# Preparation of an attention and expert kernel on one Trainium2 core: semaphores per transfer, other staging buffers, another order

## What is computed

```python
x = x + tanh(g_xattn) * xattn(layernorm(x), ctx, ctx, Wq, bq, Wk, bk, Wv, bv, Wo, bo)
# xattn: q = xn @ Wq + bq ; k = ctx @ Wk + bk ; v = ctx @ Wv + bv ; 16 heads of 32
#        softmax(q k^T / sqrt(32)) v, joined, @ Wo + bo          (ctx: 2 x 128 x 256)
x = x + tanh(g_ffn) * moe(layernorm(x))
# moe: LayerNorm with gamma, beta; logits = xn @ router_w.T; top 2 of 8 experts;
#      each expert takes up to 1280 rows: h = silu(g) * u, y = h @ w3.T, weighted and added
```

## Time and profile before

| | before |
|---|---|
| median of 3 runs | 2720.58 us (2719.67 to 2720.80) |
| the profiled execution's own time | 2716.51 us |
| its span in the trace | 2714.10 us |
| TensorE matmul busy | 2608.7 us (96%) |
| VectorE busy | 1392.1 us (51%) |
| ScalarE busy | 944.7 us (35%) |
| GpSimd busy | 410.9 us (15%) |

### The profile page before, as it was taken

The page is one execution under the profiler, slowest core; times in us unless marked ns, Lnnn a source line. Parts: engine busy times, 40 slices in busy tenths (PEclk is TensorE's granted clock), DMA queues, the critical chain, the costliest instruction groups (busy, mean ns, idle before and its releaser), DMA issues.

```text
span 2714.1 us, 40566 instructions
## 1 busy us (share of the span) xinstructions
PE 2608.7 (96%) x14166; PEld 2313.9 (85%) x14167; DVE 1392.1 (51%) x2647; ACT 944.7 (35%) x2479; POOL 410.9 (15%) x391
## 2 busy tenths in 40 slices
PE   5999999589999999999999999999999999999988
PEld 4877777489998888888988888888889999989987
DVE  4788888544444444444444444444444444445555
ACT  4766666222224222242222322232222322233343
POOL 2455555400002000020000300010000100030030
PEclk8999999799999999999999999999999999999999
DMA  7523222321103201132011321141011311033142
GB/s 266 213 78 102 94 78 97 122 111 47 46 27 77 86 24 46 47 62 86 23 46 46 63 109 46 47 113 40 30 46 39 107 47 46 33 85 118 70 126 81
DMA packets 60034, 208.38 MB, mean 77 GB/s; under 512 B 9564, under 2 KB 9836, under 8 KB 51602
## 3 DMA queue, kind: packets, MB, share of 16 engines
q1 hardware_dynamic: 43282, 175.30, 18.0%
q0 software_dynamic: 16640, 31.69, 6.1%
HBM read 145.60 MB, written 67.70 MB: 79 GB/s over the span
## 4 chain that ended last, share of the span: by engine, by line
PE 76%; issue 2%; DVE 1%; ACT 1%; DVEq 0%; DMA 0%; ACTq 0%; POOL 0%; POOLq 0%
PE bank L1540 75%; PE bank L1546 1%; DVE yacc L1480 1%; DVE slotsT_lo L1449 0%; ACT slotsT_hi L1372 0%; DVE h L1500 0%; DMA xrow<-expert_rows 0%; ACT later_hi L1368 0%; ACT yout L1396 0%; ACT h_hi L1410 0%; POOL out_dram L1354 0%; DVE w_lo L1443 0%; DVEq L1252 0%; ACT silu L1404 0%; DVEq L1479 0%
## 5 line engine op out<-in xcount | busy, mean ns | idle before, releaser
L1500 DVE TENSOR_TENSOR h<-silu,bank 128x384 f32<-128x384 f32 (+2 forms) x320 | 183.8, 574 | 826.3 <-PE bank L1540 816.8
L1540 PE MATMUL bank<-slotsT_hi,early_hi 128*128 128x384 f32 (+2 forms) x1280 | 444.6, 347 | 14.4 <-issue 12.3
L1540 PE MATMUL bank<-slotsT_hi,w_hi 128*128 128x384 f32 (+2 forms) x1280 | 442.5, 346 | 5.3 <-DVE w_lo L1443 5.3
L1540 PE MATMUL bank<-slotsT_lo,early_hi 128*128 128x384 f32 (+2 forms) x1280 | 442.5, 346 | 0.4 <-issue 0.4
L1540 PE MATMUL bank<-slotsT_lo,w_hi 128*128 128x384 f32 (+2 forms) x1280 | 442.2, 345 | 0.0
L1540 PE MATMUL bank<-slotsT_hi,early_lo 128*128 128x384 f32 (+2 forms) x1280 | 441.8, 345 | 0.0
L1540 PE MATMUL bank<-slotsT_hi,w_lo 128*128 128x384 f32 (+2 forms) x1280 | 441.1, 345 | 0.0
L1410 ACT CAST h_hi<-h 128x384 fp32r<-128x384 f32 (+2 forms) x320 | 169.2, 529 | 745.9 <-DVE h L1500 743.0
L1404 ACT ACTIVATE silu<-bank 128x384 f32<-128x384 f32 (+2 forms) x320 | 162.0, 506 | 728.8 <-PE bank L1540 728.3
L1480 DVE TENSOR_TENSOR yacc<-bank,yacc 128x512 f32<-128x512 f32 x464 | 316.6, 688 | 169.0 <-PE bank L1540 169.0
L1540 PE MATMUL bank<-later_hi,h_hi 128*128 128x512 f32 x1008 | 399.8, 397 | 0.3 <-DVE yacc L1480 0.3
(11 more groups left out here) (195 smaller groups left out, 3533.3 us busy)
## 6 DMA issues: line engine op xcount, KB each, us to landing
staged<-in_moe_w_dram SPq DMA_DIRECT2D x33, 1536.0 KB
raw<-in_moe_w_dram SPq DMA_DIRECT2D x32, 1536.0 KB, 6.4
xrow<-expert_rows SPq DMA_DIRECT2D x42, 520.0 KB, 9.0
expert_rows<-zeros SPq DMA_DIRECT2D x40, 520.0 KB, 7.5
xin<-in_x_dram SPq DMA_DIRECT2D x17, 512.0 KB, 3.7
xres<-in_x_dram SPq DMA_DIRECT2D x15, 512.0 KB, 3.7
out_dram<-xres SPq DMA_DIRECT2D x15, 512.0 KB
staged<-in_L_xattn_Wq_dram SPq DMA_DIRECT2D x1, 1024.0 KB, 10.7
```

The source lines that it names most:

```text
L1500: nc.vector.tensor_tensor(h32[q % 2][:, 0:W], silu[q % 2][:, 0:W], UB[q % 2][:, 0:W], ALU.mult)\
L1540: last = nc.tensor.matmul(out_ap, st, mv, start=(at == 0), stop=(at == n - 1))
```

## The change

Each transfer, or small group, gets its own semaphore. x of block 0 is issued first, then context, router weights and biases, `Wk`, `Wq`, `Wo`, `Wv`, `bv`, the gates. The biases are loaded as four rows of 128 into the residual's buffer and turned by PE. Raw `Wk`, `Wv` and `Wo` lie in `pT`, `Wq` alone in `probs`. `Wq` is rounded and split in four pieces. x is turned ahead of the keys; only batch 0's keys are made before the first queries, batch 1's behind them. The values are made inside block 0, batch 1's keys are split by POOL in block 0, and `Wo`'s subtraction moves to a later place in block 0.

```diff
-                    for dst, src in kv_parts:
-                        sp.dma_start(dst, src, allow_slow_non_contiguous=True).then_inc(kv_loaded, 16)
                     load_xin(0)
+                    for dst, src in ((row[:, :, 0:DI], ctx_img.rearrange("b s d -> s b d")),
...
+                                     (bias_rows[0:KD, 0, 0:P], bk.rearrange("(m p) -> m p", p=P)),
+                                     (bias_rows[0:KD, 1, 0:P], bq.rearrange("(m p) -> m p", p=P))):
+                        sp.dma_start(dst, src).then_inc(ctx_loaded, 16)
+                    sp.dma_start(wk_raw, wide(Wk)).then_inc(wk_loaded, 16)
                     sp.dma_start(wq_raw, wide(Wq)).then_inc(wq_loaded, 16)
-                    load_xres(0)
+                    sp.dma_start(wo_raw, wide(Wo)).then_inc(wo_loaded, 16)
+                    sp.dma_start(wv_raw, wide(Wv)).then_inc(wv_loaded, 16)
+                    sp.dma_start(bv_row[:, :], bv.rearrange("(a n) -> a n", a=1)).then_inc(wv_loaded, 16)
+                    for i, g in enumerate((g_xattn, g_ffn)):
+                        sp.dma_start(gates[:, i:i + 1], g.partition_broadcast(P), allow_slow_non_contiguous=True)\
+                          .then_inc(gates_loaded, 16)
+
+                    sp.wait_ge(x_ready, 2)
+                    load_xin(1)
                     for dst, src in ((gbo_b, bo), (gamma_b, ln_gamma), (beta_b, ln_beta)):
                         sp.dma_start(dst[:, :], src.partition_broadcast(P)).then_inc(late_loaded, 16)
-                    sp.wait_ge(x_ready, 2)
-                    load_xin(1)
-                    sp.wait_ge(prep_pe, 3)
-                    sp.dma_start(wo_raw, wide(Wo)).then_inc(wo_loaded, 16)
+                    load_xres(0)
...
@@ POOL
+                    for t in (k_hi[0], k_lo[0]):
+                        last = nc.gpsimd.memset(t[:, :, :].bitcast(fp32), 0.0)
+                    last.then_inc(k0_cleared, 1)
                     rstd_x(0)
+                    for t in k_hi[1:] + k_lo[1:]:
...
+                    def later_keys():
+                        pool.wait_ge(cleared, 2)
+                        pool.wait_ge(k1_biased, KD)
+                        pool.wait_ge(pn_ready, KD - 1)
+                        for i, (rows, cols) in enumerate(diagonal):
+                            nc.gpsimd.tensor_copy(k_hi[1][rows, :, cols], keys(1, rows)).then_inc(k1_rounded, 1)
+                            pool.wait_ge(k1_rounded, i + 1)
+                            nc.gpsimd.tensor_tensor(k_lo[1][rows, :, cols], keys(1, rows),
+                                                    k_hi[1][rows, :, cols].bitcast(fp32), ALU.subtract).then_inc(k1_split, 1)
...
                         if has(n, 0):
                             norm(n, 2)
+                        if isinstance(n, int) and n == 0:
+                            later_keys()
@@ ACT
                     norm_x(0)
                     act.wait_ge(wq_loaded, 16)
-                    nc.scalar.copy(wq_hi[:, :, :], wq_raw).then_inc(prep_act, 1)
+                    for k in range(KD):
+                        nc.scalar.copy(wq_hi[:, k, :], wq_raw[:, k, :]).then_inc(wq_rounded, 1)
                     x_halves(0)
...
+                    act.wait_ge(wo_loaded, 16)
+                    nc.scalar.copy(wo_hi[:, :, :], wo_raw).then_inc(wo_rounded, 1)
+                    act.wait_ge(k0_cleared, 1)
+                    act.wait_ge(k_biased, KD)
+                    for rows, cols in diagonal:
+                        nc.scalar.copy(k_hi[0][rows, :, cols], keys(0, rows)).then_inc(k_rounded, 1)
...
                     q_halves(0, 0)
+                    act.wait_ge(k_made, 2)
+                    for m in range(KD):
+                        nc.scalar.activation(row[:, 1, m * LKV:(m + 1) * LKV], bank[5][:, m * LKV:(m + 1) * LKV],
+                                             ACT.Identity, bias=bkT[:, m:m + 1], scale=SCALE).then_inc(k1_biased, 1)
@@ DVE
+                    stats_x(0)
...
+                    for m in range(KD):
+                        nc.vector.tensor_scalar(row[:, 0, m * LKV:(m + 1) * LKV], bank[4][:, m * LKV:(m + 1) * LKV],
+                                                SCALE, bkT[:, m:m + 1], ALU.mult, ALU.add).then_inc(k_biased, 1)
...
                     q_rest(0, 0)
+                    stats_x(1)
@@ PE
                     transposes_x(0)
...
+                    keys_made(0)
+                    pe.wait_ge(wq_split, 1)
                     queries(0, 0)
+                    keys_made(1)
+                    pe.wait_ge(k0_split, 1)
...
                             queries(n, 1)
+                            if isinstance(n, int) and n == 0:
+                                values_made(0)
                             scores(n, 2, b_s)
                         if has(n, 1):
...
                             transposes_x(n + 1)
+                        if isinstance(n, int) and n == 0:
+                            values_made(1)
```

More of the change, by code:

```diff
@@ L226, in flamingo_gated_layer @@
             row_of = lambda blk: spare_row if isinstance(blk, int) and blk == LAST - 1 else row
+            keys = lambda b, rows: row[rows, b, 0:KD * LKV].rearrange("p (m t) -> p m t", m=KD)
+            diagonal = [(slice(DK * hh, DK * (hh + 1)), slice(LKV * hh, LKV * (hh + 1))) for hh in range(HG)]
             def steps(eng, step):
@@ L639, in _ @@
-                    x_rest(0)
-                    dve.wait_ge(prep_pool, 1)
-                    dve.wait_ge(prep_act, 3 + B * KD)
-                    keys = lambda b, rows: row[rows, b, 0:KD * LKV].rearrange("p (m t) -> p m t", m=KD)
-                    diagonal = [(slice(DK * hh, DK * (hh + 1)), slice(LKV * hh, LKV * (hh + 1))) for hh in range(HG)]
-                    for b in range(B):
-                        for rows, cols in diagonal:
-                            last = nc.vector.tensor_copy(k_hi[b][rows, :, cols], keys(b, rows))
@@ new lines, in _ @@
+                    nc.vector.tensor_scalar(bkT[:, :], bank[2][:, KD * E:KD * E + KD], SCALE, None, ALU.mult)
+                    nc.vector.tensor_copy(bqT[:, :], bank[2][:, KD * E + KD:KD * E + 2 * KD]).then_inc(turned_read, 1)
+                    for k in range(KD):
+                        dve.wait_ge(wq_rounded, k + 1)
+                        last = nc.vector.tensor_tensor(wq_lo[:, k, :], wq_raw[:, k, :], wq_hi[:, k, :].bitcast(fp32),
+                                                       ALU.subtract)
@@ new lines, in _ @@
+                    last.then_inc(wq_split, 1)
+                    x_rest(0)
+                    dve.wait_ge(turned_read, 1)
+                    dve.wait_ge(k_made, 1)
+                    for m in range(KD):
+                        nc.vector.tensor_scalar(row[:, 0, m * LKV:(m + 1) * LKV], bank[4][:, m * LKV:(m + 1) * LKV],
+                                                SCALE, bkT[:, m:m + 1], ALU.mult, ALU.add).then_inc(k_biased, 1)
+                    for i, (rows, cols) in enumerate(diagonal):
+                        dve.wait_ge(k_rounded, i + 1)
+                        last = nc.vector.tensor_tensor(k_lo[0][rows, :, cols], keys(0, rows),
+                                                       k_hi[0][rows, :, cols].bitcast(fp32), ALU.subtract)
@@ new lines, in _, with values @@
+                    last.then_inc(k0_split, 1)
+                    q_rest(0, 0)
+                    stats_x(1)
+                    def values():
+                        for b in range(B):
+                            dve.wait_ge(v_made, b + 1)
+                            nc.vector.tensor_copy(vals[b][:, :, :], bank[2 + b][:, :].rearrange("p (h d) -> p h d", h=H))                              .then_inc(vals_ready, 1)
+                    def late_splits():
+                        dve.wait_ge(wo_rounded, 1)
@@ L923, in _, with keys_made @@
                                                    row[0:E, a, DI + c * P:DI + (c + 1) * P], ident[0:E, 0:E])
-                    last.then_inc(prep_pe, 1)
-                    pe.wait_ge(prep_dve, 1)
+                    for i in range(2):
+                        last = nc.tensor.transpose(bank[2][:, KD * E + i * KD:KD * E + (i + 1) * KD],
+                                                   bias_rows[0:KD, i, 0:P], ident[0:KD, 0:KD])
+                    last.then_inc(turned, 1)
                     ctxT = xnT
-                    for b in range(B):
+                    def keys_made(b):
                         for m in range(KD):
```

123 lines of the change are left out of this document (52 added, 71 removed).

## The result

| | before | changed |
|---|---|---|
| median | 2720.12 us (4 runs, 2715.93 to 2720.80) | 2701.39 us (4 runs, 2698.94 to 2703.30) |
| ratio to before | | 0.9938, 95% interval 0.9927 to 0.9950 |
| the profiled execution's own time | 2716.51 us | 2701.12 us |
| its span | 2714.10 us | 2698.40 us |
| first scores, fifth scores group | 35.05, 57.19 | 20.66, 36.07 |

The medians differ by 18.7 us, where 20.0 was forecast. By the ratio the gain is 16.9 us, with an interval of 13.6 to 19.9, so the forecast lies at its upper edge. The two profiled executions differ by 15.4 (their spans by 15.7), because what follows the load of block 4's x, the same code in both, took 3.2 us longer in the second; how that stretch scatters is shown at the end of the experiments.

What follows compares the result with a forecast made beforehand. The prediction took the late start, work not yet needed and DVE's key splits to bound the head, PE's work block 0; 15.0 + 6.0 - 0.8 - 0.2 = 20.0 us less, 2720.6 to 2700.6, range 2696.5 to 2709.

Steps and rivals of the forecast that it cites:

- Bound and place: Head: late start, early work for batch 1 and values, and DVE's key splits set 35.05; 15.0 saved.
- `Wq` at 9: Head: data to the end of `Wq`, 2.3 MB at 408 GB/s, there by about 9, before ACT wants it.
- The turn of x: Head, on PE ahead of batch 0's keys: takes 1.0, to 11.1.
- Which of the two ends sets the first scores: First scores: DVE's q low part ends at 19.4, PE's batch 1 keys at 20.0, so PE's sets them.
- Block 0: First scores to fifth scores group: PE's work is the length, 16.1 for 22.1, 6.0 saved if the clock stays up.
- Rival A: Half clock stays: up to 2 in the head, some 6 in block 0; about 2707.6; chance 0.10.
- Given back: `Wo`'s low part and bias row ahead of `maxima(0, 6)` cost 0.8; POOL's delay of `norm(0, 3)` costs 0.2.
- Rival B: New late work binds: `Wo`'s subtraction and POOL's eight instructions fall together; gain 13, 2707.6; chance 0.12.
- POOL's keys: Eight key instructions ahead of `norm(0, 3)`: take 7.0, bounds 6.4 to 8.4, costing 0.2 (0 to 1.6).
- The signs: PE's first instruction near 5.5, first scores near 20, fifth group near 36, no PE idle over 1 us between.
- Rival C: Gain absorbed by slow early data or 40 zero fills ahead of the first scatter; 2715 to 2720; chance 0.04.
- D: Slower: half clock at the stage change lasts into the experts, about 2726; chance 0.02.

## Why the prediction was right

By its own steps, with what the profile of the changed kernel shows:

| step | forecast | measured |
|---|---|---|
| x landed, statistics start | 4.3 | 4.64 |
| normalisation starts | 8.5 | 8.63 |
| x turned | 10.0 to 11.1 | 10.20 to 12.17 |
| `Wq` there | 9 | 11.0 |
| queries start | 14.0 | 15.52 |
| q's low part (DVE) ready | 19.4 | 20.5 |
| batch 1's keys (PE) done | 20.0 | 20.4 |
| first scores | 20.0 (15.0 saved) | 20.66 (14.4 saved) |
| to the fifth group | 16.1 (6.0 saved) | 15.41 (6.7 saved) |
| given back | 1.0 | 2.2 at block 4's x |
| saved at block 4's x | 20.0 | 18.9 |
| medians | 20.0 | 18.7 |
| the profiled executions | 20.0 | 15.4 |

The number came out closer than its parts. Up to the fifth group an error of 0.6 and one of 0.7 cancel, and that is luck. So is part of the agreement of the median, 2701.4 for 2700.6: the profiled execution was forecast at 2696.5 and took 2701.1, since the gain was 1.1 short and the tail 3.2 longer; but the distance from it to the median, kept at 4.1, was 0.3 this time. The mechanism, what each step waits for, is what held, with the exceptions below.

- **Bound and place.** Right: one wait for all transfers held the start, and to put it back costs 10.9, or some 8 if it ended as early as in the kernel before. DVE's chain ahead of q's low part was the second bound; undoing batch 1's move costs 6.2 at the first scores and 7.9 at block 4's x. These don't add up with the others (10.9 + 7.9 + 2.8 + 1.1 = 22.7, more than 18.9), since undoing one part can also drop the clock or lengthen another wait.
- **`Wq` at 9** failed: the forecast assumed the full 408 GB/s from the start, but the queues moved 164 GB/s in 6 to 7 and 289 in 7 to 8 (the data are also 2.4 MB rather than 2.3). `Wq` was there at 11.0 and ACT waited 0.9 for it. The queries started 1.5 late. Of this, 1.0 is ACT's later start on `Wq`; the rest is DVE, which was still busy with `Wq`'s low part (from 11.68 to 14.1) when ACT had the first half of x's high part, where the forecast called that work hidden. The 0.3 by which x landed late is not in it, since ACT then waited for `Wq` all the same.
- **The turn of x** was priced at 1.0 from a row at full clock; behind PE's idle it took 1.97. It ended at 12.17, ahead of ACT's cast of x at 13.11, so this cost nothing.
- **Which of the two ends sets the first scores** came out the other way. The forecast had PE's (20.0) behind DVE's (19.4). DVE's chain was 1.1 late, with the queries, and ended last (PE waited 0.26 for it). Batch 1's keys, priced at 2.8, took 1.95 at full clock, so PE was done at 20.4 though its queries started late. The 0.66 at the first scores is what is left of the two errors.
- **Block 0** was right in kind, PE's work sets its length; 16.1 was 0.7 high, mostly because its two sets of queries took 2.88 and 2.86 and not 3.1 each. The four scores groups took 3.1 together, as forecast.
- **Rival A** (half clock) did not occur where it would have cost much: only the turn of x, the first keys and the stretch behind the wait of 2.06 were slow. Its ground, that every idle stretch before was followed by half clock, went too far: PE's 1.73 idle ahead of 43.80 in the kernel before was followed by a turn at the full rate (1.09 for eight). The undoing of batch 1's keys showed half clock once PE idles 6 us. The prediction's gain counted on PE staying busy, and it did.
- **Given back.** `Wo`'s subtraction was priced at 0.8 for pushing back `maxima(0, 6)`. The size by the next block's first scores (66.10 before, 46.13 now, so 20.0 saved where 21.1 were at the fifth group) is 1.15, but the mechanism was another one: it held POOL's work and with it `norm(0, 1)`, for which PE waited 2.06; with the subtraction moved away, the wait and the 1.15 are gone (35.87 to 44.78, 8.9, for 10.06). Rival B named the two late works meeting, not this.
- **POOL's keys** were put at 7.0, with bounds of 6.4 to 8.4; they took 8.1 (46.48 to 54.53), and PE waited 0.98 for what stood behind, where 0.2 was taken off. This is the term that was most undersized. The two-input instruction took 1.28, above the 0.95 of the bounds; the sum stayed inside them only because the pauses were shorter. The prediction took the one-input cast near the clear's rate and a two-input instruction at `norm`'s; measured are 0.60 and 1.28. The rule that it weighed against this, the Trainium skill's "GPSIMD Engine Reference", Engine selection (two inputs about twice as slow as on VectorE, one input about equal), gave an estimate of 8.2 and was the nearer one. The trace agrees for two inputs, 1.28 against VectorE's 0.69, 1.9 times; for one input it has 0.60 against 0.42, 1.4 times and not equal.
- **The range** reached down to 2696.5 by a gain of 24, which its own terms don't give: without any cost from POOL and DVE it is 21.0, and batch 1's keys at full clock add 0.6 at most, since DVE's 19.4 then ends last.
- **The signs.** First scores, fifth group, the end of `norm(0, 3)` and PE's wait under 1 us for it came as said. PE's first work was at 6.40 and not 5.5, and it idled 1.99 ahead of the turn of x, where under 1 was said.
- **Rival C** (gain absorbed) and **D** (slower) did not occur. Behind block 4's x PE's named waits up to 450 us are 8.7 for q's low part and 4.1 for the router's counts before, 8.7 and 4.6 after.

## What to carry to other kernels

Microseconds at a kernel's head reach its end one for one, within the scatter of what follows, if the rest is bound by one engine without absolute times: give each first transfer its own semaphore, issue what the longest chain needs first, and put work that no one needs yet into a stretch where the bound engine would wait. Where late work must go somewhere, look not only for idle time on its own engine but at what runs beside it, since VectorE and GpSimd can stop each other. Compare small changes by the time of one early instruction in the trace, which repeated within 0.1 to 0.5 us in two pairs here, when the median scatters by several; and look at the granted clock ahead of it, which alone moved it by 1.0.

## What was not expected of the hardware

- VectorE and GpSimd held each other up, in full. Beside a subtraction with two SBUF inputs (2.24) POOL's 0.20 took 1.61 and its 1.90 took 3.83; beside POOL's `norm`, VectorE's scaling of a row in SBUF took 2.09 for 0.47. The subtraction, which came first each time, kept its 2.24. The Trainium skill ("GPSIMD Engine Reference", Specifications) names this contention for VectorE instructions with two SBUF inputs or in a two-port mode. The trace agrees for the subtraction; whether the scaling ran in such a mode no row shows. Its form here, by the ends: the one that comes second does nearly all of its work once the other has ended. `norm` ends 1.8 behind the subtraction, the scaling 0.3 behind `norm`. POOL's key instructions kept 0.60 and 1.26 to 1.30 beside VectorE's maxima and splits that read PSUM.
- A tail of 2,617 us of identical instructions varied from 2614.0 to 2624.5 from one execution to the next. Between three profiles the difference sits in one stretch of half clock that lasted 3.4, 6.8 or 10.2 us.
- The price of 1,024 transfers of 4 bytes was 1.4 us, half of what the rates beside them had suggested.
